# Normalising the second rows on VectorE, quantising layer 1 later, and both halves of a unit's probabilities on GpSimd one slot later

## The chip, the cores and the metric

The kernel runs on one core of one Trainium2 chip. The metric is the device time in microseconds (us). Before the change it is 1662.19 us, the median of 3 runs (1658.11 to 1663.67).

## What is computed

`x` is 32 batches of 256 rows by 256 features (float32); `ctx_768` has 77 context rows of 192 features for each batch. Two layers follow each other, each with an attention on the context and a feed-forward part. The feed-forward part of layer 0 is a gated one with integer weights; that of layer 1 quantises its rows to 8-bit integers.

```python
x = x + L0_xattn(_layernorm(x), ctx, Wq, Wk, Wv, Wo, bo)   # 16 heads of 64
x = x + L0_ffn(_layernorm(x), w_gate, w_up, w_down)        # 768 hidden, silu(gate) * up
x = x + L1_xattn(_layernorm(x), ctx, Wq, Wk, Wv, Wo, bo)
x = x + L1_ffn(_layernorm(x), rhs)
# L1_ffn(lhs): s = max|lhs| / 127 by row, r = max|rhs| / 127 by column
#              (round(lhs / s) @ round(rhs / r)) * s * r
```

## The kernel before, in words

A first part of some 200 us computes keys and values of all batches and both layers and stores them in DRAM. Then `h` runs over 64 steps (`NB`, layer 0 of the 32 batches, then layer 1 of the same), and two more for what is left. A step is one batch of one layer, in four slots `u` (called `UNITS`); a unit is four heads. In `lay`, `lay[d]` is the layer of step `h + d`, so that `lay[-2] == 0` means work that belongs to the batch two steps back, in layer 0. Each engine has its own `body` with the whole order of its slots written out by hand, and counting semaphores between the engines; no engine looks ahead past its next instruction.

What one unit k passes through:

- TensorE, slot k: the scores into one PSUM tile `SC`, once ScalarE has read those of the unit before (L1200). In the same slot it makes the queries of the unit two further on (L328), projects the unit four back into `OA` (L326, L328, once VectorE's `oT_l` is there) and weighs the values of the unit three back (L1234).
- VectorE, slot k: `maxima` of half 0 and of half 1 (L1507; a half is 128 of the 256 rows).
- ScalarE, slot k: `exponentials` of both halves (L1379) into `ex[k % 2]`, which must have been read by GpSimd two units before.
- VectorE: `reciprocals` of half 0 at the end of slot k, of half 1 at the start of slot k+1 (L1512).
- GpSimd: `probabilities`, three operations a half: `pr` = ex times reciprocal (L1668), its fp16 part `p` (L1681), the low part (L1673). Half 0 comes late in slot k, half 1 early in slot k+1. A half's `p` is turned by a DMA transpose that SyncE issues (L1090, L1091), in slot k+1.

At the end of slot 3, VectorE adds the residual and makes `x1` (L1648), the rows behind the attention. Before it may overwrite the old `x1` in layer 0 it waits for GpSimd's copy of it into `y` (L1710). Then the second rows are made: `spreads` and `moments` of `x1` on VectorE (L365, L371, L373, which gives `ve`), `inverse` on GpSimd (`rs`, L388), `shift` on VectorE (`nmr`, L378), `normalise` on ScalarE in two activations (`x2`, L347). In layer 0, ScalarE then takes the fp16 part (L343), VectorE the low part (L357, `x<-x`), SyncE turns both (L1099), and TensorE multiplies by the gate and up weights. GpSimd also takes the low part of four of six hidden tiles (`low_hidden`, L1659), adds the bias to `x_res` in layer 0 (L1692) and makes the inverses of the first and third norms.

In layer 1 the second rows go to VectorE's `am` (L1595, largest magnitude), `quantising_scale` (L1500, L1503), ScalarE's `q_a` (L1425), VectorE's `q_i` (L1588), TensorE's turn (L319), VectorE's `qiT` (L1615), TensorE's `quantised`, VectorE's `ya` (L1600) and `yo` (L1634), and a store of SyncE (L1151).

SyncE's queue is one list too: per step it holds eight transposes of `p`, two loads of keys (`load_keys`, L302: units 2 and 3 in slot 0, units 0 and 1 of the next batch in slot 2), two of values, the residual, and in layer 0 further transposes and stores. An issue waits behind all that are written before it.

## Time and profile before

| | us |
|---|---|
| median of 3 runs | 1662.19 |
| lowest and highest | 1658.11, 1663.67 |
| the profiled execution's own time | 1661.49 |
| its span in the trace | 1659.7 |
| granted TensorE clock, mean | 0.994 |

In the profile PE is TensorE's matmuls and PEld its weight loads (which overlap PE), DVE is VectorE, ACT ScalarE, POOL GpSimd, SP SyncE. A row gives the line of the kernel, the engine, the operation, output and inputs by name (buffer numbers left out) and the count. "Idle before" is the time for which the engine stood still just before the instruction, with what released it. The ends of matmuls are modelled, and neighbouring instructions of an engine may overlap by some 0.1 us, so that distances from start to start are the ones to add.

### The profile page before, as it was taken

How to read it: one execution, taken by the hardware profiler on the slowest of the kernel's cores; microseconds unless marked ns; L12 is line 12 of the kernel's file. 1: busy time of each engine (PE TensorE's matmuls, PEld its weight loads, DVE VectorE, ACT ScalarE, POOL GpSimd, SP SyncE). 2: the span in 40 equal slices, each digit the busy share in tenths (PEclk: the TensorE clock that was granted, in tenths of full speed). 3: DMA queues.
4: the chain of work that ended last, by engine and by line, in shares of the span. 5: the costliest groups of instructions: out<-in, count | busy, mean ns of one | idle time of the engine just before them, and what ended most of it. 6: DMA issues, size and time to landing. Idle time of an engine off the chain costs nothing.

```text
span 1659.7 us, 74850 instructions
## 1 busy us (share of the span) xinstructions
PE 1520.7 (92%) x27282; PEld 1318.8 (79%) x27282; DVE 1344.1 (81%) x3522; ACT 1372.0 (83%) x5640; POOL 1254.1 (76%) x1893
## 2 busy tenths in 40 slices
PE   7999889999999999999999999899999988999995
PEld 4556569889889889889889888777777777777774
DVE  6777668888888888888888878788888878888886
ACT  6656688888888888898898888888888888888884
POOL 5100288889889889889898888788888887888884
PEclk9999999999999999999999999999999999999998
DMA  9997699877787778778778988888888888888995
GB/s 260 348 307 263 193 205 175 170 171 179 163 171 180 164 169 179 163 170 176 170 168 176 163 171 153 163 180 176 177 183 185 184 178 177 181 175 176 178 186 112
DMA packets 740022, 307.78 MB, mean 185 GB/s; under 512 B 629201, under 2 KB 725361, under 8 KB 737841
## 3 DMA queue, kind: packets, MB, share of 16 engines
q1 hardware_dynamic: 738049, 299.32, 81.8%
q0 software_dynamic: 1840, 6.82, 1.4%
q8 instruction: 68, 1.11, 0.3%
q14 instruction: 65, 0.53, 0.1%
HBM read 87.09 MB, written 65.54 MB: 92 GB/s over the span
## 4 chain that ended last, share of the span: by engine, by line
ACT 23%; PE 21%; POOL 19%; DVE 11%; issue 10%; DMA 2%; SPq 1%; ACTq 1%; DVEq 0%; POOLq 0%
ACT ex L1379 15%; PE psum L328 14%; POOL pr L1668 6%; POOL p L1681 4%; ACT x L347 4%; PE psum L1234 3%; PE psum L1200 3%; DVE x L1648 2%; POOL p L1673 2%; DVE nmax L1507 2%; POOL hT_l L1659 2%; POOL rs L388 2%; POOL x_res L1692 2%; ACT q_a L1425 1%; DVE st L365 1%
## 5 line engine op out<-in xcount | busy, mean ns | idle before, releaser
L1379 ACT ACTIVATE ex<-psum,nmax 128x77 f32<-128x77 f32 x2048 | 636.3, 331 | 73.5 <-DVE nmax L1507 70.6
L1379 ACT ACTIVATION_READ_ACCUMULATOR ex<-psum,nmax 128x1 f32 x2048 | 432.5, 211 | 0.0
L1673 POOL TENSOR_TENSOR p<-pr,p 128x308 f16<-128x308 f32 x512 | 397.3, 776 | 38.5 <-ACT p L343 0.3
L1668 POOL TENSOR_TENSOR pr<-ex,rden 128x308 f32<-128x308 f32 x512 | 366.1, 715 | 67.1 <-DVE rden L1512 66.9
L328 PE MATMUL psum<-xT,wq_h 128*64 128x256 f16 x4064 | 353.0, 275 | 0.0
L328 PE MATMUL psum<-wo_h,oT_h 128*64 128x256 f16 x1792 | 249.6, 274 | 47.8 <-DVE oT_l L357 47.6
L1681 POOL CAST p<-pr 128x308 f16<-128x308 f32 x509 | 253.1, 497 | 38.2 <-DMA pT<-p 5.8
L328 PE MATMUL psum<-xT,wq_l 128*64 128x256 f16 x2032 | 280.8, 273 | 0.0
L1507 DVE TENSOR_REDUCE nmax<-psum 128x4 f32<-128x308 f32 x512 | 235.7, 461 | 22.5 <-PE psum L1200 20.6
L328 PE MATMUL psum<-wo_l,oT_h 128*64 128x256 f16 x1792 | 248.2, 273 | 0.0
L328 PE MATMUL psum<-wo_h,oT_l 128*64 128x256 f16 x1792 | 248.1, 273 | 0.0
L328 PEld LDWEIGHTS psum<-xT,wq_h 128*64 128x64 f16 x4064 | 211.0, 110 | 12.1
L1234 PE MATMUL psum<-pT,vb 77*64 77x256 f16 x3072 | 212.5, 273 | 0.0
L343 ACT ACTIVATE oT_h<-psum 128x512 f16<-128x512 f32 x256 | 152.5, 596 | 44.1 <-PE psum L1234 39.7
L357 DVE TENSOR_TENSOR oT_l<-psum,oT_h 128x512 f16<-128x512 f32 x256 | 174.5, 682 | 1.5 <-ACT oT_h L343 1.5
L360 DVE SCALAR_TENSOR_TENSOR qT_l<-psum,qT_h 128x512 f16<-128x512 f32 x256 | 173.6, 678 | 0.0
L1234 PEld LDWEIGHTS psum<-pT,vb 77*64 77x64 f16 x3072 | 167.2, 110 | 3.8 <-issue 0.4
L1200 PEld LDWEIGHTS psum<-kb,qT_h 64*128 64x128 f16 x4096 | 113.1, 94 | 65.4 <-issue 65.4
L1200 PE MATMUL psum<-kb,qT_h 64*128 64x77 f16 x4096 | 145.3, 197 | 11.3 <-ACT ex L1379 5.0
L343 ACT ACTIVATE qT_h<-psum 128x512 f16<-128x512 f32 x256 | 152.3, 595 | 2.9 <-PEq L398 2.9
L328 PEld LDWEIGHTS psum<-wo_h,oT_h 128*64 128x64 f16 x1792 | 102.2, 110 | 65.5 <-DVE oT_l L357 58.0
L388 POOL TENSOR_TENSOR rs<-ve,half_neg 128x2 f32<-128x2 f32 x127 | 88.4, 696 | 76.6 <-DVE ve L373 73.6
(164 smaller groups left out, 3484.2 us busy)
## 6 DMA issues: line engine op xcount, KB each, us to landing
keys<-ks SPq DMA_DIRECT2D x16, 1232.0 KB, 7.2
kb<-keys SPq DMA_DIRECT2D x256, 77.0 KB, 2.8
vb<-vals SPq DMA_DIRECT2D x128, 154.0 KB
vals<-vs SPq DMA_DIRECT2D x64, 256.0 KB, 4.0
x_pair<-in_x_dram SPq DMA_DIRECT2D x32, 256.0 KB, 3.0
pT<-p SPq DMA_TRANSPOSE x512, 3.3
x_res<-in_x_dram SPq DMA_DIRECT2D x32, 256.0 KB, 3.1
mid_x<-y SPq DMA_DIRECT2D x32, 256.0 KB, 2.4
```

Source lines behind the costliest of these rows:

```text
L328: last = pe.matmul(o[b * DH:(b + 1) * DH], w[:, b * DH:(b + 1) * DH], x, **flags)
L343: return act.activation(dst, src, ACT.Copy, scale=scale)
L357: return dve.tensor_tensor(dst, src, hi, ALU.subtract)
L360: return dve.scalar_tensor_tensor(out=qT_l[i][:, :, :], in0=src, scalar=Q_DOWN, in1=qT_h[i][:, :, :], op0=ALU.mult, op1=ALU.subtract)
L388: pool.tensor_tensor(rs[:, :], ve[:, :], half_neg[:, :], ALU.pow).then_inc(s_inv[k], 1)
L1200: last = pe.matmul(SC[:, b, at], w[rows, a, t * P:(t + 1) * P], kb[u // 2][rows, b, part, u % 2 * PPU + a, :], start=(q == 0), stop=(q == ...
L1234: last = pe.matmul(o[b * DH:(b + 1) * DH, a, :].rearrange("p (t q) -> p t q", q=P), vb[u // 2][:, part, c:c + DH], pT[u][0:NK, b, at:at + ...
L1379: last = act.activation(ex[i][:, t, b, :], SC[:, t, b * NK:(b + 1) * NK], ACT.Exp, bias=nmax[i][:, t, b:b + 1], accum_out=den[i][:, t, b:b ...
L1507: dve.tensor_reduce(nmax[i][:, t, :], SC[:, t, :].rearrange("p (h k) -> p h k", k=NK), AX_X, ALU.max, negate=True).then_inc(s_m, 1)
L1668: pool.tensor_tensor(pr[:, t, :, :], ex[i][:, t, :, :], r, ALU.mult).then_inc(s_p, 1)
L1673: pool.tensor_tensor(d[:, t, 1, :, 0:NK], pr[:, t, :, :], d[:, t, 0, :, 0:NK], ALU.subtract).then_inc(s_pl, 1)
L1681: pool.tensor_copy(p16[v % 2][:, t, 0, :, 0:NK], pr[:, t, :, :]).then_inc(s_ph, 1)
```

## The change

Five edits go together.

1. VectorE normalises the second rows itself, out of `mv` and `rs`, in two operations a batch, in both layers (`normalise_rows`). The `shift` on VectorE and the two activations on ScalarE go.
2. Layer 1's quantising moves later: `spreads` and `moments` of its `x1` go behind both maxima of slot 0, the normalising and `am` from slot 0 to slot 1, `q_a` and `q_i` from slot 1 to slot 2 (`q_a` ahead of the slot's queries and exponentials on ScalarE), the turn from slot 1 to slot 2, `quantised`, `ya` and `yo` from slot 2 to slot 3, the store to slot 0 of the next step. `x1` also waits for `yo`.
3. One reciprocal a unit, of both halves, at the start of slot k+1.
4. GpSimd does half 0 of unit k at the start of slot k+1 too, then half 1.
5. In layer 0 `inverse` of the second rows stays the last of slot 3 on GpSimd, right behind the copy into `y`, and half 0 of unit 3, which stood between the two, comes after it.

```diff
+        def normalise_rows(dve, k, dst, src, mv, rs, count, s_done):
+
+            dve.wait_ge(s_inv[k], count)
+            dve.sem_inc(s_stgo[k], 1)
+            for t in range(QT):
+                dve.tensor_scalar(dst[:, t, :], src[:, t, :], mv[:, t, 0:1], rs[:, t:t + 1], ALU.subtract,
+                                  ALU.mult).then_inc(s_done, 1)
...
@@ SyncE
+                        if u == 0 and lay[-3] == 1:
+                            store_output(h - 3 - B)
                         if u == 0 and lay[1] == 0 and like >= 4:
                             turn_rows(sp, h + 1, like + 1)
...
-                        if u == 3 and lay[-2] == 1:
-                            sp.wait_ge(s_ysum, h - 1 - B)
-                            sp.dma_start(batch_of(out_rows, b_out), yo[:, :, :]).then_inc(s_yo, 16)
@@ TensorE
-                        if u == 2 and lay[-2] == 1:
+                        if u == 3 and lay[-2] == 1:
                             pe.wait_ge(s_qe, h - 1 - B)
                             for t in range(QT):
                                 quantised(t, bank("quant", t))
...
-                        if u == 1 and lay[-2] == 1:
+                        if u == 2 and lay[-2] == 1:
                             pe.wait_ge(s_qi, h - 1 - B)
                             turn(pe, as_f16(bank("turned_q", 0)), q_i).then_inc(s_qt, 1)
@@ ScalarE
+                        if u == 2 and lay[-2] == 1 and like <= NB:
+                            act.wait_ge(s_li, h - 1 - B)
+                            after(act, s_qi, h - 2 - B)
+                            for t in range(QT):
+
+                                act.activation(q_a[:, t, :], x2[:, t, :], ACT.Copy, scale=linv[:, t:t + 1],
+                                               bias=MAGIC).then_inc(s_qa, 1)
...
-                        if u == 0 and lay[-2] is not None and like <= NB:
-                            act.wait_ge(s_nmr[1], h - 1)
-                            if lay[-2] == 0 or like == B + 2:
-                                after(act, s_x216l, h - 2)
-                            normalise(act, x2, x1, rs2, 1, s_x2)
@@ VectorE
-                    def reciprocals(k, i, t):
-                        dve.wait_ge(s_e, QT * k + t + 1)
-                        dve.reciprocal(rden[i][:, t, :], den[i][:, t, :]).then_inc(s_r, 1)
+                    def reciprocals(k, i):
+                        dve.wait_ge(s_e, QT * k + 2)
+                        dve.reciprocal(rden[i][:, :, :], den[i][:, :, :]).then_inc(s_r, 1)
...
+                        if u == 0 and lay[-2] == 1:
+                            dve.wait_ge(s_x1, h - 1)
+                            spreads(dve, x1, st2, s_st2)
                             moments(dve, 1, st2, mv2, ve2, s_st2, s_mv2, h - 2)
...
-                        if u == 0 and lay[-2] is not None and like <= NB:
-                            shift(dve, 1, mv2, rs2, h - 1)
+                        if u == 0 and lay[-2] == 0:
+                            normalise_rows(dve, 1, x2, x1, mv2, rs2, h - 1, s_x2)
...
+                        if u == 1 and lay[-2] == 1 and like <= NB:
+                            normalise_rows(dve, 1, x2, x1, mv2, rs2, h - 1, s_x2)
...
-                        if lay[0] is not None:
-                            reciprocals(n + u, u % 2, 0)
...
+                            if lay[-2] == 1:
+                                dve.wait_ge(s_ysum, h - 1 - B)
@@ GpSimd
                     for u in range(UNITS):
                         if u == 0 and lay[-3] == 0:
                             low_hidden(2, h - 3)
+                        if lay[(u - 1) // UNITS] is not None and (like, u) != (NB, 0):
+                            probabilities(h + (u - 1) // UNITS, (u - 1) % UNITS, 0)
...
-                        if (like, u) == (NB - 1, 3):
-                            weights_of(h, 3, 0)
-                            low_of(h, 2, 1)
-                        elif lay[0] is not None:
-                            probabilities(h, u, 0)
...
-                        if u == 3 and lay[-1] == 0:
+                        if u == 3 and lay[-1] is not None:
                             inverse(pool, 1, ve2, rs2, h)
```

## Rows read from the trace of the kernel before

**Rows 1.** The page, first part: busy time, share of the span, instructions.

```profile
PE 1520.7 (92%) x27282; PEld 1318.8 (79%) x27282; DVE 1344.1 (81%) x3522; ACT 1372.0 (83%) x5640; POOL 1254.1 (76%) x1893
```

**Rows 2.** L1648 (x1), in 300 to 900 and 1100 to 1600: min/median/max ns, first, last start.

```profile
L1648 DVE SCALAR_TENSOR_TENSOR x<-psum,x_res x24: 690/692/693, 308.3 to 886.9; 128x512 f32<-128x512 f32 x24
...
L1648 DVE SCALAR_TENSOR_TENSOR x<-psum,x_res x26: 690/692/692, 1105.0 to 1594.3; 128x512 f32<-128x512 f32 x26
```

**Rows 3.** Who waited for whom, 300 to 900 us (layer 0): total us, times, longest.

```profile
PE psum L328 <- DVE oT_l L357: 25.7, 24, 1.2
...
POOL hT_l L1659 <- ACT hT_h L343: 27.7, 24, 1.2
...
POOL rs L388 <- DVE ve L373: 12.1, 24, 0.8
```

**Rows 4.** The same view, 1100 to 1600 us (layer 1).

```profile
PE psum L319 <- DVE q_i L1588: 19.5, 25, 0.8
...
PE psum L326 <- DVE oT_l L357: 17.2, 25, 0.7
...
PE psum L328 <- DVE oT_l L357: 10.0, 26, 0.4
```

**Rows 5.** GpSimd in order of time, layer 0: start us, us, what, idle before.

```profile
609.03 0.61 POOL L1710 COPY y<-x 128x512 f32<-128x512 f32 x1
609.62 0.70 POOL L1668 TENSOR_TENSOR pr<-ex,rden 128x308 f32<-128x308 f32 x1
...
612.40 0.69 POOL L388 TENSOR_TENSOR rs<-ve,half_neg 128x2 f32<-128x2 f32 x1 [0.74 <-DVE ve L373]
...
629.20 0.89 POOL L1681 CAST p<-pr 128x308 f16<-128x308 f32 x1
...
634.41 0.61 POOL L1710 COPY y<-x 128x512 f32<-128x512 f32 x1
```

**Rows 6.** VectorE in order of time, layer 0.

```profile
629.11 0.69 DVE L357 TENSOR_TENSOR x<-x_pair,x 128x512 f16<-128x512 f32 x1
...
635.16 0.69 DVE L1648 SCALAR_TENSOR_TENSOR x<-psum,x_res 128x512 f32<-128x512 f32 x1 [0.24 <-POOL y L1710]
...
637.27 0.17 DVE L373 TENSOR_SCALAR ve<-mv 128x2 f32<-128x2 f32 x1
```

**Rows 7.** Groups of instructions by form, 300 to 900 us: count, busy us, mean ns.

```profile
L1681 POOL CAST p<-pr 128x308 f16<-128x308 f32 x191 | 104.7, 548 | 12.3
...
L378 DVE SCALAR_TENSOR_TENSOR nmr<-mv,rs 128x2 f32<-128x2 f32 x71 | 30.7, 432 | 4.6 <-POOL rs L388 4.6
```

**Rows 8.** L767, the one earlier use of VectorE's normalising form.

```profile
L767 DVE TENSOR_SCALAR x_pair<-x_pair,mv,rs x2: 404/405/406, 166.3 to 166.6; 128x256 f32<-128x256 f32 x2
```

**Rows 9.** ScalarE in order of time, both layers: normalising and q_a.

```profile
614.66 1.09 ACT L347 ACTIVATE x<-x,nmr,rs 128x256 f32<-128x256 f32 x2
...
1309.76 0.91 ACT L1425 ACTIVATE q_a<-x,linv 128x256 f32<-128x256 f32 x2
```

**Rows 10.** TensorE in order of time, layer 1: first scores of slots 1, 2, 3 and 0.

```profile
1305.76 0.25 PE L1200 MATMUL psum<-kb,qT_h 64*128 64x77 f16 x4
...
1312.53 0.25 PE L1200 MATMUL psum<-kb,qT_h 64*128 64x77 f16 x4
...
1316.89 0.24 PE L1200 MATMUL psum<-kb,qT_h 64*128 64x77 f16 x4
...
1320.83 0.24 PE L1200 MATMUL psum<-kb,qT_h 64*128 64x77 f16 x4
```

**Rows 11.** SyncE's queue in order of time, and landing of the keys, layer 1.

```profile
1311.82 1.24 SPq L1091 DMA_TRANSPOSE pT<-p  x1
1313.11 1.23 SPq L302 DMA_DIRECT2D kb<-keys  x2
...
DMA to landing us min/median/max: 2.3/2.8/4.3
```

**Rows 12.** One batch of layer 1: busy us of PE, PEld, DVE, ACT, POOL; clock; DMA.

```profile
1300.71:1320.28 19.57, 17.69 (x344) 15.41 (x342) 15.88 (x41) 16.80 (x79) 15.95 (x26) 1.00 0.80 180
```

More of the change, by code:

```diff
@@ L1004, in uses @@
                         out.append(("gu", 0))
-                    if lay[-2] == 1:
-                        out.append(("turned_q", 0))
                 if u == 2:
@@ L1009, in uses @@
                         out.append(("down", 0))
-                    if lay[-2] == 1:
-                        out += [("quant", 0), ("quant", 1)]
                     if lay[-3] == 0:
@@ L1015, in uses @@
                         out.append(("gu", 1))
+                    if lay[-2] == 1:
+                        out.append(("turned_q", 0))
+                if u == 3 and lay[-2] == 1:
+                    out += [("quant", 0), ("quant", 1)]
                 if u == 3 and lay[-2] == 0:
@@ L1419, in body @@
                             exponentials(n + u, u % 2, 0)
-                        if u == 1 and lay[-2] == 1 and like <= NB:
-                            act.wait_ge(s_li, h - 1 - B)
-                            after(act, s_qi, h - 2 - B)
-                            for t in range(QT):
-                                act.activation(q_a[:, t, :], x2[:, t, :], ACT.Copy, scale=linv[:, t:t + 1],
-                                               bias=MAGIC).then_inc(s_qa, 1)
                         if u == 1 and lay[1] == 1:
@@ L1531, in body @@
                         if lay[(u - 1) // UNITS] is not None:
-                            reciprocals(n + u - 1, (u - 1) % 2, 1)
+                            reciprocals(n + u - 1, (u - 1) % 2)
                         if lay[0] is not None:
                             maxima(n + u, u % 2, 0)
-                        if u == 0 and lay[-2] is not None:
+                        if u == 0 and lay[-2] == 0:
+                            moments(dve, 1, st2, mv2, ve2, s_st2, s_mv2, h - 2)
+                        if u == 2 and lay[-2] == 0:
+                            hidden(0, h - 2)
+                        if u == 2 and lay[-3] == 0:
+                            out_rows(0)
+                        if u == 2 and lay[2] == 0:
+                            shift(dve, 0, mv1, rs1, h + 2)
+                        if lay[-1] is not None:
+                            dve.wait_ge(s_oh, n + u - 3)
+                            low(dve, oT_l[u % 2][:, :, :], weighed(like, u), oT_h[u % 2][:, :, :]).then_inc(s_ol, 1)
+                        if u == 2 and lay[-2] == 1:
+                            dve.wait_ge(s_qa, QT * (h - 1 - B))
+                            after(dve, s_qt, h - 2 - B)
+                            dve.tensor_scalar(q_i[:, :, :], q_a[:, :, :], MAGIC + INT8_MAX, MAGIC,
+                                              ALU.min, ALU.subtract).then_inc(s_qi, 1)
+                        if lay[0] is not None:
+                            maxima(n + u, u % 2, 1)
+                        if u == 0 and lay[-2] == 1:
+                            dve.wait_ge(s_x1, h - 1)
+                            spreads(dve, x1, st2, s_st2)
                             moments(dve, 1, st2, mv2, ve2, s_st2, s_mv2, h - 2)
@@ L1553, in body @@
                                                   ALU.add).then_inc(s_qa, 1)
-                        if u == 2 and lay[-2] == 0:
-                            hidden(0, h - 2)
-                        if u == 2 and lay[-3] == 0:
-                            out_rows(0)
-                        if u == 2 and lay[2] == 0:
-                            shift(dve, 0, mv1, rs1, h + 2)
-                        if lay[-1] is not None:
-                            dve.wait_ge(s_oh, n + u - 3)
-                            low(dve, oT_l[u % 2][:, :, :], weighed(like, u), oT_h[u % 2][:, :, :]).then_inc(s_ol, 1)
-                        if lay[0] is not None:
-                            maxima(n + u, u % 2, 1)
                         if late_tile(like, u) is not None:
@@ L1584, in body @@
                             sigmoid_gate(4, h - 3)
-                        if u == 1 and lay[-2] == 1:
-                            dve.wait_ge(s_qa, QT * (h - 1 - B))
-                            after(dve, s_qt, h - 2 - B)
-                            dve.tensor_scalar(q_i[:, :, :], q_a[:, :, :], MAGIC + INT8_MAX, MAGIC,
-                                              ALU.min, ALU.subtract).then_inc(s_qi, 1)
                         if lay[(u + 1) // UNITS] is not None:
@@ L1607, in body @@
                                 turned_rows(like + 1, 0)).then_inc(s_xl, 1)
-                        if u == 1 and lay[-1] == 1:
+                        if u == 1 and lay[-2] == 1 and like <= NB:
+                            dve.wait_ge(s_x2, QT * (h - 1))
+                            dve.tensor_reduce(am[:, :], x2[:, :, :], AX_X, ALU.max,
+                                              apply_absolute_value=True).then_inc(s_am, 1)
+                            quantising_scale(h - 2 - B)
+                        if u == 2 and lay[-1] == 1:
                             dve.wait_ge(s_xr, 16 * h)
@@ L1611, in body @@
                             dve.tensor_tensor(x_res[:, :, :], x_res[:, :, :], bias, ALU.add).then_inc(s_xb, 1)
-                        if u == 1 and lay[-2] == 1:
+                        if u == 2 and lay[-2] == 1:
                             dve.wait_ge(s_qt, h - 1 - B)
```

27 lines of the change are left out of this document (12 added, 15 removed).

## The prediction

> **What bounds the kernel now.** The page comes first: TensorE is busy for 92% of the span, ScalarE 83%, VectorE 81%, GpSimd 76% [rows 1]. Shares of the whole hide that there are two stages with different work a step, so the next look is at the starts of x1, one a step. In layer 0 they lie (886.9 - 308.3) / 23 = 25.16 us apart, in layer 1 (1594.3 - 1105.0) / 25 = 19.57 us [rows 2]. Some 31 steps run at the first pace and some 28 at the second, so a microsecond a step is worth about 30 us.
>
> Then the waits, stage by stage. In layer 0 TensorE stands still for 25.7 / 24 = 1.07 us a step, for VectorE's oT_l [rows 3]. But it isn't what closes the loop: GpSimd hardly ever rests. It waits 1.15 us a step for a hidden tile of ScalarE and 0.50 us for ve [rows 3], so its own work, gaps included, is 25.16 - 1.65 = 23.5 us a step. And x1 of each step stands until GpSimd has copied the old x1 into y: 0.24 us of idle with that releaser [rows 6]. The reader is to see a ring there: the copy into y, x1, statistics, ve, GpSimd's inverse, and round GpSimd's list to the next copy.
>
> In layer 1 no copy is made. There TensorE's three waits are 0.75 us for q_i, 0.66 us and 0.38 us for oT_l (19.5, 17.2 and 10.0 over 26 steps) [rows 4]: 1.80 us a step, and without them a step is 17.77 us, in line with 17.69 us of busy TensorE [rows 12].
>
> **Part by part, layer 0.** *Normalising.* ScalarE loses a pair of 1.09 us [rows 9], VectorE loses a shift of 0.43 us [rows 7] and gains two operations of the form of 0.40 us, whose starts lie 0.3 us apart [rows 8], so 0.3 to 0.4 us net. As the pair stands ahead of the fp16 part of the rows, of oT_h and of the hidden tile, these come about 1 us earlier against x1. That takes away TensorE's 1.07 us and GpSimd's 1.15 us as causes. The four reciprocals that go give VectorE 0.1 us each, as it isn't the bound: nothing.
>
> *GpSimd's order.* This is the part that costs. Before, between the copy into y and the inverse stood half 0 of unit 3: from 609.62 until the idle of 0.74 us that ends at 612.40, so 2.04 us [rows 5]. In this time VectorE made x1 and its statistics: the copy ends at 634.41 + 0.61 = 635.02, ve at 637.27 + 0.17 = 637.44 [rows 5, 6], 2.4 us, and in the batch before, copy to inverse took 612.40 - 609.64 = 2.76 us [rows 5]. The half covered it but for 0.50 us on average. After the change the inverse stands right behind the copy. The copy holds up x1, x1 holds up ve, ve holds up the inverse, and GpSimd's whole list of the next step, half 0 of unit 3 first, is queued behind it. GpSimd rests 2.4 to 2.8 us a step, and the step is its work plus this rest: 23.5 + 2.5 = 26.0 us, where 2.5 us is the half's 2.04 plus the mean wait of 0.50. That is +0.84 us a step, and over 31 steps **+26 us**. Below, it could be +0.4 if fewer of GpSimd's operations meet VectorE's (a cast takes 0.89 us beside a VectorE subtraction, 0.548 us on average [rows 5, 6, 7]); above, +1.1 from 2.76 us, and more under the third rival.
>
> What is late behind it: probabilities of unit 3 by about 4 us against x1, the other units less. Their values are weighed three slots, some 18 us, later, and two GpSimd passes stand between a buffer of ex and its next use. I take nothing for it. TensorE gains slack of 2 us a step that the loop doesn't let it use.
>
> On the SBUF port the trace shows that cast of 0.89 us, begun at 629.20 within VectorE's subtraction of 629.11 [rows 5, 6]. The Trainium skill, GPSIMD Engine Reference, section Specifications, says that GpSimd's SBUF interfaces are shared with VectorE and contend with its instructions that have two SBUF inputs or run in a 2-port mode. The trace agrees for the two inputs; by the rule the added normalising would speak against this change, and the third rival prices it.
>
> **Layer 1.** *ScalarE's pair and the early wait.* VectorE no longer stands for x2 ahead of slot 1's maxima, and its statistics come behind both maxima of slot 0, so that oT_l of slots 0 and 1 is ready before TensorE asks: 0.38 + 0.66 us. q_i is now made a slot earlier than TensorE turns it, which takes 0.75 us. Full worth 1.80 us.
>
> *What q_a costs at its new place.* The distances of the scores are 6.77 us for slot 1, 4.36 for slot 2, 3.94 for slot 3 [rows 10], and 19.57 less these for slot 0, 4.50. Slot 3 is what maxima, 16 exponential instructions and two fp16 copies allow, since TensorE may write the next scores only after them. In slot 2, q_a comes between these: 0.8 to 0.91 us [rows 9] makes 4.65 to 4.85, against TensorE's own some 4.3 there (quantised leaves, a turn of about the same length comes). So 0.4 us a step is handed back: 17.77 + 0.4 = 18.15 us, -1.42 us a step, over 28 steps **-40 us**. Bounds: -1.80 (q_a fits) and -0.67 (the second rival). quantised in slot 3 and the turn in slot 2 are work of equal length moved: nothing. yo and the extra wait of x1 for it lie on VectorE's own list, ahead of x1 already, and there x1 had to wait for TensorE anyway: nothing. The store goes behind one transpose in slot 0 of the next step and delays the values' load by its issue, about 0.6 us; values are used two slots on.
>
> *GpSimd in layer 1.* Its 15.95 us [rows 12] and gaps, some 17, fit into 18.15, but ve now comes behind both maxima and unit 3 waits behind the inverse. An estimate, from the start of slot 0's scores: 0.6 us for them, 1.4 for VectorE's two maxima and oT_l, 1.2 for statistics and ve (of the 2.4 above, without x1 and one of the maxima), so ve at 3.2 us, the inverse until 3.9, and halves of 2.0 us: half 0 of unit 0, the third, ends at 9.9 us, half 1 at 11.9. In SyncE's queue the keys of the next batch's first units stand behind that half's transpose. I get 13.2 us for their issue (11.9 plus 1.24 [rows 11]), their second load 0.6 later, landing 2.8 us on, so 16.6 us of 18.15: covered by 1.5 us.
>
> **Ends.** At the change of layers steps are of mixed kind; nothing. At the last step GpSimd finds two more operations of 0.7 to 0.75 us behind the last reciprocal: +1.5 us.
>
> **Sum.** Against the profiled execution's own 1661.5 us (0.7 below the median of 1662.19): 1661.5 + 26 - 40 + 1.5 = **1649 us**. About 0.3%, 5 us, is what a measurement of this kernel tells from no change.
>
> **Rivals.** *First, TensorE is the bound in both layers.* The Trainium skill, Perfetto Trace Analysis, section Identifying the Most-Contended Engine, calls the engine of highest occupancy the one to work on (for TensorE by weight loads rather than by matmul time). Worked from rows, the mechanism is that the loop through GpSimd has play that I don't see, and layer 0 gives back TensorE's 1.07 us: -33 us there, -1.80 x 28 = -50 in layer 1, 1580 us. For it: TensorE's 92%. Against it: x1's wait for the copy, and GpSimd's list, whose order leaves nothing to hide 2.5 us. Chance 0.08.
>
> *Second, the other side: the keys come late.* Place: SyncE's queue in slot 1 and 2 of layer 1. If a half takes GpSimd 2.2 us in place of 2.0 (0.8 us by half 1 of unit 0) and the keys land at the slow end, 4.3 us [rows 11], the first scores wait until 16.6 + 0.8 + 1.5 = 18.9 us. Layer 1 gains 0.67 x 28 = 19 us, layer 0 loses 26: 1661.5 + 26 - 19 + 1.5 = 1670 us. It decides from the point where a step of layer 1 is longer than 19.57 - 26/28 = 18.6 us. For it: a DMA share of 0.80 [rows 12] that rises as the step shrinks. Against it: the median landing. Chance 0.12.
>
> *Third, port contention.* Each normalising pair meets GpSimd in its fullest stretch and lengthens it by its own 0.6 to 0.7 us: 21 us more in layer 0, 1670 us. For it: that cast; against it: a form that has no case beside a busy GpSimd. Chance 0.10.
>
> **Numbers.** The forecast has 0.60, with 1632 to 1662 as its own range (layer 0 +12 to +34, layer 1 -50 to -32). The remaining 0.10 is for layer 0 losing less than bounded, or a gain of layer 1 that stops at q_i alone, 0.75 us. Range 1620 to 1673: it leaves out the first rival. Faster by over 0.3%: 0.69 (most of the forecast, the first rival, a little of the rest); within 0.3%: 0.12; slower: 0.19 (second and third rival without their mild cases).
>
> **What would show it.** In layer 0: x1 starts 26.0 us apart; GpSimd idle 2.4 to 2.8 us before its inverse, for ve, in every step, and no more for the hidden tile; VectorE's x1 waiting for the copy by over 0.5 us. In layer 1: starts 18.15 us apart, no wait of TensorE for q_i, slot 2 longer than TensorE's work, ScalarE's q_a without idle ahead of it. I am wrong if layer 0's distance falls, if TensorE waits for the keys, or if GpSimd's casts grow beside the normalising pair.

## The result: slower by 1.9%, and the profile after

| | before | after |
|---|---|---|
| median, us | 1661.41 (4 runs) | 1691.93 (4 runs) |
| lowest and highest | 1658.11 to 1663.67 | 1688.96 to 1700.91 |
| ratio | | 1.0194, 95% interval 1.0149 to 1.024 |
| profiled execution: time, span | 1661.49, 1659.7 | 1688.96, 1687.2 |

The forecast was 1649 us. The change makes the kernel slower by 30 us, and the time lies above the range. The page of the changed kernel, first part (busy us, share, instructions), beside [rows 1]:

```profile
PE 1536.4 (91%) x27282; PEld 1318.8 (78%) x27282; DVE 1396.8 (83%) x3329; ACT 1314.8 (78%) x5514; POOL 1265.3 (75%) x1893
```

ScalarE is relieved by 57 us and VectorE loaded with 53 us more, although it has 193 instructions fewer. Shares still say little; the distances of x1 say where the time is. x1 of the changed kernel, in 300 to 900 us and in 1130 to 1630 us (min/median/max ns, first and last start), beside [rows 2]:

```profile
L1659 DVE SCALAR_TENSOR_TENSOR x<-psum,x_res x23: 690/691/692, 311.3 to 889.1; 128x512 f32<-128x512 f32 x23
...
L1659 DVE SCALAR_TENSOR_TENSOR x<-psum,x_res x26: 691/692/693, 1135.8 to 1619.5; 128x512 f32<-128x512 f32 x26
```

Layer 0: (889.1 - 311.3) / 22 = 26.26 us a step, forecast 26.0. Layer 1: (1619.5 - 1135.8) / 25 = 19.35 us, forecast 18.15. All 63 distances added up, the first 34 (layer 0 and the change of layers) grew from 854.6 to 886.2 us, +31.6; the other 29 went from 562.9 to 559.0 us, -3.9. The first x1 comes 0.2 us earlier, and the stretch behind the last is the same, 11.4 us. So layer 0 lost what was forecast and a little more, and layer 1 gave 4 us where 40 were forecast.

**Layer 0.** Waits of the changed kernel, 300 to 900 us (total us, times, longest), beside [rows 3]:

```profile
POOL rs L396 <- DVE ve L381: 69.0, 46, 2.5
...
DVE x L1659 <- POOL y L1725: 31.6, 23, 1.4
```

GpSimd in order of time, one turn of the ring (start us, us, what, idle before), beside [rows 5], and VectorE in the same stretch, beside [rows 6]:

```profile
619.96 1.07 POOL L396 TENSOR_TENSOR rs<-ve,half_neg 128x2 f32<-128x2 f32 x1 [0.50 <-DVE ve L381]
...
625.74 0.61 POOL L1725 COPY y<-x 128x512 f32<-128x512 f32 x1
628.85 0.69 POOL L396 TENSOR_TENSOR rs<-ve,half_neg 128x2 f32<-128x2 f32 x1 [2.50 <-DVE ve L381]
```

```profile
626.49 0.69 DVE L1659 SCALAR_TENSOR_TENSOR x<-psum,x_res 128x512 f32<-128x512 f32 x1 [1.38 <-POOL y L1725]
...
628.60 0.17 DVE L381 TENSOR_SCALAR ve<-mv 128x2 f32<-128x2 f32 x1
```

The reader sees the ring as the prediction drew it: copy 625.74, x1 626.49, ve 628.60, inverse 628.85, and nothing of GpSimd's between copy and inverse. GpSimd rests 2.50 us there in every step, its wait for the hidden tile is gone, and x1 waits 1.38 us for the copy. There is one rest more, 0.50 us ahead of another inverse in the list, that of the third norm: 69.0 / 23 = 3.0 us a step in all.

**Layer 1.** Waits of the changed kernel, 1130 to 1630 us, beside [rows 4]:

```profile
POOL rs L396 <- DVE ve L381: 42.5, 26, 1.7
...
DVE nmax L1513 <- PE psum L1211: 36.6, 55, 1.7
...
PE psum L328 <- DVE oT_l L357: 20.6, 46, 0.6
ACT q_a L1424 <- DVE linv L1509: 20.1, 23, 0.9
```

TensorE's wait for q_i is gone, as forecast, and for the keys it waited a single time, 0.7 us. But VectorE now stands 36.6 / 26 = 1.4 us a step for scores, waits that were 0.2 us before, and yet is late elsewhere. VectorE in order of time at the seam of two steps of layer 1:

```profile
1344.87 0.48 DVE L1513 TENSOR_REDUCE nmax<-psum 128x4 f32<-128x308 f32 x1 [0.53 <-PE psum L1211]
...
1346.85 0.86 DVE L1604 SCALAR_TENSOR_TENSOR ya<-psum,lsc,rhs_sb 128x256 f32<-128x256 f32 x2
1347.84 1.27 DVE L1643 TENSOR_TENSOR yo<-ya,x 128x512 f32<-128x512 f32 x1
1349.25 0.69 DVE L1659 SCALAR_TENSOR_TENSOR x<-psum,x_res 128x512 f32<-128x512 f32 x1
...
1350.31 0.68 DVE L357 TENSOR_TENSOR oT_l<-psum,oT_h 128x512 f16<-128x512 f32 x1
```

and TensorE's first scores of slot 3 and then of slots 0, 1, 2 and 3 of the next step, beside [rows 10]:

```profile
1344.25 0.25 PE L1211 MATMUL psum<-kb,qT_h 64*128 64x77 f16 x4 [0.32 <-ACT ex L1390]
...
1348.62 0.24 PE L1211 MATMUL psum<-kb,qT_h 64*128 64x77 f16 x4
...
1353.52 0.25 PE L1211 MATMUL psum<-kb,qT_h 64*128 64x77 f16 x4 [0.32 <-DVE qT_l L360]
...
1358.16 0.24 PE L1211 MATMUL psum<-kb,qT_h 64*128 64x77 f16 x4
...
1363.76 0.25 PE L1211 MATMUL psum<-kb,qT_h 64*128 64x77 f16 x4 [0.40 <-ACT ex L1390]
```

ya and yo fill VectorE from 1346.85 to 1349.11. x1 starts right behind them, without any wait for TensorE, 0.63 us after the scores of slot 0 have begun, and oT_l and the maxima of slot 0 stand behind x1. Before, x1 had waited for TensorE.

The same rows tell where in the step the time went. From score to score, slot 0 lasts 4.90 us here, slot 1 4.64 and slot 2 5.60. The medians over layer 1 are 4.75, 4.64, 5.53 and 4.37 us for slots 0 to 3, against 4.50, 6.77, 4.37 and 3.93 before. So slot 1 gave 2.1 us; slot 2, into which the quantising moved, took 1.2 us of it back, slot 3 0.4 and slot 0 0.25.

### The profile page after: what moved, and what is told of

Read it like the earlier page. It is cut to its first block, busy times and chain, and to the rows that moved or that the text cites. A ratio compares the mean times of both kernels' runs of the same rounds, so it can differ in the third digit from the quotient of the medians.

```text
span 1687.2 us, 74557 instructions
## 1 busy us (share of the span) xinstructions
PE 1536.4 (91%) x27282; PEld 1318.8 (78%) x27282; DVE 1396.8 (83%) x3329; ACT 1314.8 (78%) x5514; POOL 1265.3 (75%) x1893
## 3 DMA queue, kind: packets, MB, share of 16 engines
q8 instruction: 68, 1.11, 0.3%
## 4 chain that ended last, share of the span: by engine, by line
POOL 42%; issue 25%; DVE 11%; PE 3%; ACT 3%; DMA 2%; SPq 1%; DVEq 0%; POOLq 0%; ACTq 0%
POOL pr L1679 16%; POOL p L1692 10%; POOL p L1684 6%; POOL hT_l L1670 4%; POOL x_res L1705 2%; POOL rs L396 2%; ACT ex L1390 2%; DVE nmax L1513 2%; DVE oT_l L357 2%; DVE qT_l L360 2%; PE psum L328 1%; DMA pT<-p 1%; DVE yo L1643 1%; PE psum L1211 1%; POOL y L1725 1%
## 5 line engine op out<-in xcount | busy, mean ns | idle before, releaser
L1679 POOL TENSOR_TENSOR pr<-ex,rden 128x308 f32<-128x308 f32 x512 | 380.3, 743 | 20.7 <-DVE rden L1518 20.4
L1692 POOL CAST p<-pr 128x308 f16<-128x308 f32 x509 | 246.4, 484 | 36.5 <-DMA pT<-p 4.0
L396 POOL TENSOR_TENSOR rs<-ve,half_neg 128x2 f32<-128x2 f32 x127 | 98.0, 772 | 185.5 <-DVE ve L381 185.4
L1245 PEld LDWEIGHTS psum<-pT,vb 77*64 77x64 f16 x3072 | 165.0, 110 | 15.8 <-issue 13.0
```

The source lines that it names most:

```text
L396: pool.tensor_tensor(rs[:, :], ve[:, :], half_neg[:, :], ALU.pow).then_inc(s_inv[k], 1)
L1245: last = pe.matmul(o[b * DH:(b + 1) * DH, a, :].rearrange("p (t q) -> p t q", q=P), vb[u // 2][:, part, c:c + DH], pT[u][0:NK, b, at:at + ...
L1679: pool.tensor_tensor(pr[:, t, :, :], ex[i][:, t, :, :], r, ALU.mult).then_inc(s_p, 1)
L1692: pool.tensor_copy(p16[v % 2][:, t, 0, :, 0:NK], pr[:, t, :, :]).then_inc(s_ph, 1)
```

## The experiments

In the expectations, R is the theory that the ring of layer 0 sets its step, V that VectorE's list sets that of layer 1, Q that q_a's place does. The table has the mean distance of x1, in steps 4 to 26 (layer 0) and 37 to 60 (layer 1), and the ratio to the kernel before where both were timed several times; the others have the one time of their profiled execution.

| kernel | layer 0 | layer 1 | us | ratio, interval |
|---|---|---|---|---|
| before | 25.16 | 19.57 | 1661.41 | |
| after | 26.27 | 19.34 | 1691.93 | 1.0194, 1.0149 to 1.024 |
| e1 after, GpSimd's old order | 24.55 | 19.08 | 1640.85 | 0.9876, 0.9848 to 0.9904 |
| e2 before, GpSimd's new order | 26.09 | 19.57 | 1693.27 | 1.019, 1.0158 to 1.0221 |
| e3 after, copy ahead of half 1 | 25.53 | 19.34 | 1674.41 | 1.0084, 1.0056 to 1.0113 |
| e4 after, no normalising in layer 1 | 26.30 | 18.12 | 1660.84 | |
| e5 after, that pair twice | 26.27 | 20.04 | 1719.76 | |
| e6 after, no yo | 26.27 | 18.81 | 1677.63 | |
| e7 after, q_a behind exponentials | 26.27 | 19.32 | 1694.35 | 1.0211, 1.0167 to 1.0255 |
| e8 e1, bias on GpSimd | 24.56 | 19.07 | 1638.80 | 0.9857, 0.9834 to 0.9879 |
| e9 e1, layer 1's pair on ScalarE | 24.59 | 19.91 | 1661.94 | 0.9987, 0.9973 to 1.0001 |
| e10 e1, layer 0's pair on ScalarE | 25.16 | 19.06 | 1655.41 | |
| e11 before, edit 1 alone | 24.55 | 18.30 | 1608.58 | 0.9651, 0.9614 to 0.9689 |
| e12 before, edit 1 in layer 0 alone | 24.56 | 19.57 | 1646.66 | 0.9873, 0.9833 to 0.9912 |
| e13 e11, product and yo in slot 3 | 24.58 | 19.16 | 1634.80 | |
| e14 e11, statistics late | 24.58 | 20.50 | 1678.80 | |
| e15 e1, statistics early | 24.56 | 19.39 | 1645.95 | |

### GpSimd's order: e1, e2, e3

e1 undoes edits 3, 4 and 5 in the changed kernel.

```diff
-                        if lay[(u - 1) // UNITS] is not None and (like, u) != (NB, 0):
-                            probabilities(h + (u - 1) // UNITS, (u - 1) % UNITS, 0)
+                        if u == 3 and lay[-1] == 1:
+                            inverse(pool, 1, ve2, rs2, h)
+                        elif lay[0] is not None:
+                            probabilities(h, u, 0)
...
+                        if lay[0] is not None:
+                            reciprocals(n + u, u % 2, 0)
```

> The changed kernel with GpSimd's old order and the two old reciprocals a unit; normalising on VectorE and the later quantising stay. Theory R (a ring in layer 0: copy into y, x1, ve, inverse, with nothing of GpSimd's between copy and inverse): layer 0 falls from 26.27 us a step to 24.2 to 24.7, since half 0 of unit 3 stands between them again and ScalarE's pair is gone. Theory P (the normalising pair beside a busy GpSimd costs layer 0 its time): layer 0 stays over 25.5. Layer 1 by both near 19.4, because its limit is thought to be VectorE's list. In all 1625 to 1645 us by R, over 1665 by P.

e2 is the other side: the kernel before with edits 3 to 5 alone.

> The kernel before with GpSimd's new order and one reciprocal a unit, and nothing else. R: layer 0 goes from 25.14 to about 26.0 us a step, GpSimd resting some 2.5 us ahead of the inverse of the second rows. P: layer 0 stays within 0.2 us of 25.14. Layer 1: its inverse comes at once after slot 3, unit 3 waits behind it: 19.6 to 19.9 us a step. In all 1685 to 1700 us by R, 1660 to 1670 by P.

e1: layer 0 fell to 24.55 us, 1.72 us below the changed kernel, and the whole is faster than before. e2: the new order alone gives +0.93 us a step in layer 0, nothing in layer 1, and a ratio of 1.019, the whole slowdown. The only wait of GpSimd in layer 0 (300 to 900 us of e2) is the one for ve, twice a step as in the changed kernel:

```profile
POOL rs L388 <- DVE ve L373: 69.0, 46, 2.5
```

The order is the cause in layer 0; both sides agree. They move edits 3, 4 and 5 together, and no run parts the single reciprocal from the order of GpSimd's list.

e3 keeps the new order but puts the copy into y one half earlier, so that a half stands between copy and inverse again.

```diff
+                        if u == 3 and lay[-2] == 0:
+                            ...
+                            pool.tensor_copy(y[:, :, :], x1[:, :, :]).then_inc(s_yx, 1)
                         if (like, u) == (NB - 1, 3):
                             weights_of(h, 2, 1)
```

> The changed kernel with one move: in slot 3 of layer 0 GpSimd copies x1 into y ahead of half 1 of unit 2, so that this half stands between copy and inverse. R: layer 0 falls from 26.27 to 24.2 to 24.8 us a step and GpSimd rests at most 0.6 us before that inverse. P: it stays over 25.8. Layer 1 as in the changed kernel, 19.4. In all 1625 to 1650 us by R.

25.53 us: a miss. The rest ahead of the second norm's inverse fell only from 2.50 to 1.63 us. GpSimd and TensorE of e3, order of time and waits, 300 to 900 us:

```profile
622.94 0.69 POOL L396 TENSOR_TENSOR rs<-ve,half_neg 128x2 f32<-128x2 f32 x1 [1.63 <-DVE ve L381]
```

```profile
PE psum L328 <- POOL hT_l L1670: 17.6, 23, 0.8
```

With the halves a slot later in GpSimd's list, its low part of a hidden tile comes later too, and TensorE's down projection waits 0.77 us a step for it, a wait that the kernel before doesn't have (the changed kernel has it too, 16.6 / 22 = 0.75 us). The chain of waits of e3 goes from there over the third norm to the copy into y. So the order binds in a second place, which the prediction did not name. That this second loop sets e3's 25.53 us is read from the chain; no run took it away.

### Layer 1 as a sum of VectorE's work: e4 to e8

The theory at this point: VectorE's list bounds layer 1, and what was added to it costs its length. e4 leaves out layer 1's normalising (am and q_a read x1 itself), e5 does the pair a second time into a buffer of its own, e6 leaves out the addition of x1 to layer 1's product.

```diff
 e5
+                            for t in range(QT):
+                                dve.tensor_scalar(x2b[:, t, :], x1[:, t, :], mv2[:, t, 0:1], rs2[:, t:t + 1],
+                                                  ALU.subtract, ALU.mult).then_inc(s_dbl, 1)
 e6
-                            dve.tensor_tensor(yo[:, :, :], ya[:, :, :], x1[:, :, :], ALU.add).then_inc(s_ysum, 1)
+                            dve.sem_inc(s_ysum, 1)
```

> The changed kernel without the normalising of the second rows of layer 1 (row maximum and quantising read x1 itself), all waits kept. Theory V (VectorE's list bounds layer 1): a step of layer 1 falls from 19.4 us by most of the pair's 1.2 to 1.4 us, to 18.0 to 18.5. Theory Q (the place of q_a on ScalarE ahead of slot 2's exponentials, or the keys, bound it whatever VectorE does): it falls by less than 0.5 us. Layer 0 unchanged at 26.27.

> The changed kernel with the normalising pair of layer 1 done twice, the first time into a tile of its own. V (VectorE's list bounds layer 1, and a pair beside GpSimd takes 1.2 to 1.4 us): a step of layer 1 goes from 19.35 to 20.5 to 20.8 us. If the pair's port contention were not what costs it (uncontended pair, 0.7 us): 20.0. Theory Q (VectorE isn't the bound): under 19.8.

> The changed kernel without yo, the addition of x1 to layer 1's product (the product alone is stored); ya and all waits stay. V: the 1.27 us that yo takes ahead of x1 go from VectorE's list; a step of layer 1 falls from 19.35 by 0.5 to 1.2 us, and x1 starts right behind TensorE's projection. Q: under 0.3 us.

Without the pair layer 1 is 1.22 us faster, without yo 0.53 us; with the pair twice 0.70 us slower, half of what the theory asked. Part of the asymmetry lies in lsc, an operation of 128x2, behind the pair: groups of 1130 to 1630 us in the changed kernel, of 1150 to 1600 in e4 and in e5:

```profile
L368 DVE TENSOR_SCALAR x<-x,mv,rs 128x256 f32<-128x256 f32 x52 | 35.5, 721 | 0.0
L1643 DVE TENSOR_TENSOR yo<-ya,x 128x512 f32<-128x512 f32 x26 | 29.7, 1143 | 3.1
...
L1506 DVE TENSOR_SCALAR lsc<-am 128x2 f32<-128x2 f32 x26 | 16.4, 632 | 0.9
```

```profile
L1645 DVE TENSOR_TENSOR yo<-ya,x 128x512 f32<-128x512 f32 x25 | 19.9, 795 | 3.0
...
L1506 DVE TENSOR_SCALAR lsc<-am 128x2 f32<-128x2 f32 x24 | 4.3, 180 | 0.8
```

```profile
L1508 DVE TENSOR_SCALAR lsc<-am 128x2 f32<-128x2 f32 x23 | 3.9, 170 | 0.8
```

lsc is 0.63 us in the changed kernel and 0.17 to 0.18 us in both others: they shift it against GpSimd's work. yo falls from 1.14 to 0.80 us in e4 as well. The last section comes back to that.

e7 puts q_a behind the first exponentials of slot 2 (q_i and the turn follow it down), e8 gives layer 1's bias (0.80 us) to GpSimd in e1.

```diff
 e7
-                        if u == 2 and lay[-2] == 1 and like <= NB:
-                            ... q_a ahead of the slot's queries
                             exponentials(n + u, u % 2, 0)
+                        if u == 2 and lay[-2] == 1 and like <= NB:
+                            ... q_a
 e8
-                        if u == 2 and lay[-1] == 0:
+                        if u == 2 and lay[-1] is not None:
```

> The changed kernel with q_a behind the first four exponentials of slot 2 on ScalarE, q_i behind the slot's low part of the queries on VectorE, and the turn behind the weighing on TensorE. Q (q_a, which waits 0.87 us for its scale ahead of the queries' copy and all exponentials of slot 2, costs layer 1 its time): a step falls from 19.35 to 18.3 to 18.7 us. V: by at most 0.3 us.

> The kernel of e1 (old order of GpSimd) with layer 1's bias of x_res on GpSimd in slot 2, as in layer 0, in place of VectorE. V: VectorE's list is 0.7 to 0.9 us shorter and GpSimd's rest of 1.3 us takes most of the 1.27 us it gets: a step of layer 1 falls from 19.08 to 18.3 to 18.7 us, in all 1618 to 1632 us. Q: unchanged at 19.1, or longer if GpSimd's list of 18.3 us comes to bound it.

e7: 19.32 against 19.34 us. q_a's wait for its scale, and its place ahead of the first exponentials, cost nothing. But e7 leaves q_a in slot 2, between the exponentials of its two halves, and slot 2 stays at 5.48 us (median); what quantising in that slot costs, e7 does not say. e8: 19.07 against 19.08 us, a miss. 0.8 us of VectorE's work taken out of slot 2 changes nothing, while the pair of slot 1 and yo of slot 3 counted. So it isn't the sum of VectorE's list that bounds layer 1; the part of it that lies in certain slots counts. e8 says one thing more: GpSimd's work grew by 0.8 us a step and its wait for ve shrank as much, so GpSimd had play in layer 1 of e1 and wasn't what closed its loop.

### Who should normalise: e9 and e10

e9 takes e1 and gives layer 1's pair back to ScalarE, late; the scale, q_a, q_i and the turn come later too. e10 takes e1 and gives layer 0's pair back.

```diff
 e9, in ScalarE's body, behind the second exponentials of slot 1
+                        if u == 1 and lay[-2] == 1 and like <= NB:
+                            act.wait_ge(s_nmr[1], h - 1 - B)
+                            ...
+                            normalise(act, x2, x1, rs2, 1, s_x2)
```

> e1 (GpSimd's old order, the two old reciprocals) with layer 1's normalising given back to ScalarE, but at its new, late time: the shift of the mean on VectorE in slot 1, the two activations at the end of slot 1 behind the exponentials, the largest magnitude and the scale on VectorE in slot 2, q_a behind the first exponentials of slot 2, q_i and the turn later in the slot. All of the computation is done. Theory V, VectorE's list bounds layer 1: a pair of 1.4 us leaves it and a shift of about 0.4 us comes; by the 1.23 us a step that leaving the pair out gave, less 0.4 us for the shift, layer 1's step goes from 19.08 to 18.0 to 18.5 us, layer 0 stays at 24.5, and the whole is 1615 to 1630 us. Theory S, ScalarE is full once VectorE is relieved: the pair of 1.1 us on it comes between two slots' exponentials and the step stays at 19.0 or more, 1640 us and up.

> e1 with layer 0's normalising given back to ScalarE (shift on VectorE, two activations on ScalarE, as before the change). If the gain of e1 in layer 0 (25.16 to 24.55 us a step) is the normalising on VectorE, as the prediction had it, this kernel's layer 0 is at 25.1 to 25.2 us and layer 1 at 19.1, about 1659 us. If the gain comes from elsewhere, such as layer 1's edits or the order of VectorE's list, layer 0 stays at 24.5 to 24.7 us and the whole at 1641 us.

e10: 25.16 us, to the hundredth the distance of the kernel before. Edit 1 is worth 0.61 us a step in layer 0.

e9: layer 1 went up to 19.91 us. The number that theory S named was reached, but ScalarE is not full: it is busy for 403.8 of 480 us in layer 1 (1120 to 1600 us), in e1 for 400.4. VectorE of e9 in order of time, a little over one step:

```profile
1349.54 0.69 DVE L1666 SCALAR_TENSOR_TENSOR x<-psum,x_res 128x512 f32<-128x512 f32 x1
...
1360.81 0.68 DVE L1559 TENSOR_REDUCE am<-x 128x2 f32<-128x512 f32 x1
...
1363.10 0.90 DVE L1609 TENSOR_SCALAR q_i<-q_a 128x512 f16<-128x512 f32 x1 [0.52 <-ACT q_a L1436]
...
1365.03 0.41 DVE L1631 TENSOR_SCALAR qiT<-psum 128x512 f16<-128x512 f16 x1
...
1368.23 0.91 DVE L1614 SCALAR_TENSOR_TENSOR ya<-psum,lsc,rhs_sb 128x256 f32<-128x256 f32 x2 [0.69 <-PE psum L328]
...
1369.27 0.69 DVE L1650 TENSOR_TENSOR yo<-ya,x 128x512 f32<-128x512 f32 x1
1370.10 0.69 DVE L1666 SCALAR_TENSOR_TENSOR x<-psum,x_res 128x512 f32<-128x512 f32 x1
```

x1, statistics, normalising, am, scale, q_a, q_i, turn, qiT, product, ya, yo and then x1 of the next step: since x1 waits for yo, the whole quantising of a batch must fit into one step. Made late at its start, the chain is waited for at its end: TensorE waits for q_i in every step, 24.9 / 23 = 1.1 us (1120 to 1600 us). The wait of ya for the product, 0.69 us in the step shown, occurs in only 4 steps. Theory V fell. Of S, it is not shown that ScalarE's time bounds the step; whether the pair costs by standing between the exponentials of two slots, or by making the chain late, e9 does not part. What the run points to is edit 2 itself, which made that chain end at x1.

### Edit 2 taken apart: e11 to e15

e11 is the kernel before with edit 1 alone, in both layers, e12 the same in layer 0 only.

```diff
 e11
-                            act.wait_ge(s_nmr[1], h - 1)
-                            ...
-                            normalise(act, x2, x1, rs2, 1, s_x2)
...
-                            shift(dve, 1, mv2, rs2, h - 1)
+                            normalise_rows(dve, 1, x2, x1, mv2, rs2, h - 1, s_x2)
```

> The kernel before, with edit 1 alone, in both layers: VectorE normalises the second rows, where its shift stood in slot 0; the order of layer 1's quantising, the reciprocals and GpSimd's order stay as before. All of the computation is done. Layer 0: the prediction's first part says that TensorE's wait of 1.07 us and GpSimd's of 1.15 us for the hidden tile go; by e1 and e10 the step comes to 24.5 to 24.6 us. Layer 1: the pair costs VectorE 1.4 us a step and saves it the stand for ScalarE's pair of 1.1 us, so by theory V without edit 2 the step is 19.4 to 19.8 us, and edit 2 is worth some 0.5 us of e1's 19.08. If instead edit 2 is what costs in layer 1 (a longer chain through the quantising now that x1 waits for yo), layer 1 comes to 18.6 us or less here, and the whole under 1620 us. Theory V: 1640 to 1655 us.

> The kernel before, with edit 1 alone and in layer 0 only; layer 1 is as before the change in every instruction. All of the computation is done. If the two layers are independent, layer 0 is at 24.5 to 24.6 us a step and layer 1 at 19.57, about 1643 to 1648 us; edit 2 with its late quantising would then be worth only what e1 has beyond that, 5 us or less. If layer 0's gain in e1 needed the late quantising too, layer 0 stays at 25.1 us and the time at 1661 us.

e11 is the fastest kernel of the study: 1608.58 us, ratio 0.9651. Layer 1 is at 18.30 us without edit 2, against 19.08 us with it, so edit 2 **costs** 0.78 us a step where the prediction had counted on it for most of its gain. The two layers are independent: e12 has 24.56 and 19.57 us. Waits of layer 1 in the kernel before (1110 to 1580 us) and in e11 (1110 to 1560 us):

```profile
DVE am L1595 <- ACT x L347: 33.9, 24, 1.4
...
PE psum L319 <- DVE q_i L1588: 18.8, 24, 0.8
```

```profile
DVE x L1651 <- PE psum L328: 14.5, 24, 0.6
...
PE psum L328 <- DVE oT_l L365: 9.3, 24, 0.4
PE psum L319 <- DVE q_i L1591: 8.1, 25, 0.6
```

VectorE's wait of 1.4 us for ScalarE's pair is gone, q_i comes earlier by it, and TensorE's wait for it falls from 0.8 to 0.3 us. That is the gain the prediction wanted from a later slot; normalising on VectorE gives it by itself.

Which part of edit 2 costs? e13 moves only the product, ya and yo to slot 3 of e11, with x1's wait for yo; e14 moves only the statistics behind both maxima; e15 takes e1 and moves the statistics back.

```diff
 e13, the same in TensorE's, SyncE's and VectorE's bodies
-                        if u == 2 and lay[-2] == 1:
+                        if u == 3 and lay[-2] == 1:
...
                             after(dve, s_x2, QT * (h - 1))
+                            if lay[-2] == 1:
+                                dve.wait_ge(s_ysum, h - 1 - B)
 e14
                             maxima(n + u, u % 2, 1)
+                        if u == 0 and lay[-2] == 1 and like <= NB:
+                            dve.wait_ge(s_x1, h - 1)
+                            spreads(dve, x1, st2, s_st2)
+                            moments(dve, 1, st2, mv2, ve2, s_st2, s_mv2, h - 2)
```

> e11 (the kernel before with edit 1 alone; layer 1 at 18.30 us a step) with one part of edit 2: quantised, ya and yo go from slot 2 to slot 3, x1 waits for yo, and the store goes to slot 0 of the next step. Everything else of layer 1's quantising stays where it was. All of the computation is done. Theory Y, what costs is that ya and yo, over 2 us of VectorE's time with the gaps, stand in slot 3 ahead of x1, on which slot 0's product waits: layer 1 goes to 18.8 to 19.1 us. Theory T (the statistics' place) and theory N (the pair's place in slot 1) say that it stays at 18.2 to 18.4 us.

> e11 with another part of edit 2: layer 1's statistics of x1 (spreads and moments) go behind both maxima of slot 0, the normalising stays in slot 0 behind them. All of the computation is done. Theory T, the late ve makes GpSimd wait before its inverse and passes this on through its list: layer 1 at 18.8 us or more. Theories Y and N: 18.2 to 18.5 us.

> e1 (all of edits 1 and 2, GpSimd's old order; layer 1 at 19.08 us) with the statistics of layer 1 back at their old place ahead of slot 0's maxima; the rest of edit 2 stays. All of the computation is done. Theory T: layer 1 falls to 18.3 to 18.5 us. Theories Y and N: it stays at 18.9 to 19.2 us, as the rest of edit 2 is still there. If e13 stays at 18.3 and this kernel at 19, the pair's and the quantising's later place is what costs (theory N).

e13: 19.16 us, +0.86. That part alone costs as much as all of edit 2. VectorE of e11 and then of e13 in slots 2 and 3:

```profile
1318.24 0.86 DVE L1603 SCALAR_TENSOR_TENSOR ya<-psum,lsc,rhs_sb 128x256 f32<-128x256 f32 x2
...
1319.23 0.97 DVE L1637 TENSOR_TENSOR yo<-ya,x 128x512 f32<-128x512 f32 x1
...
1320.33 0.48 DVE L1510 TENSOR_REDUCE nmax<-psum 128x4 f32<-128x308 f32 x1
```

```profile
1314.58 0.18 DVE L1518 RECIPROCAL rden<-den 128x4 f32<-128x4 f32 x1 [0.97 <-ACT ex L1390]
1315.33 0.48 DVE L1513 TENSOR_REDUCE nmax<-psum 128x4 f32<-128x308 f32 x1 [0.57 <-PE psum L1211]
...
1317.30 0.87 DVE L1606 SCALAR_TENSOR_TENSOR ya<-psum,lsc,rhs_sb 128x256 f32<-128x256 f32 x2
...
1318.30 0.69 DVE L1640 TENSOR_TENSOR yo<-ya,x 128x512 f32<-128x512 f32 x1
1319.13 0.69 DVE L1656 SCALAR_TENSOR_TENSOR x<-psum,x_res 128x512 f32<-128x512 f32 x1
```

In e11 ya and yo fill the end of slot 2. In e13 VectorE idles there, 0.97 + 0.57 us, and slot 3 holds 1.83 us more ahead of x1 (1317.30 to 1319.13). In e11 x1 waits 14.5 / 24 = 0.60 us for TensorE, so slot 3 had no more than that to give; 1.83 - 0.60 = 1.2 us more than it could hide, of which 0.86 us came out in the step. e13 also moves TensorE's product, some 0.6 us of matmuls, to slot 3 ahead of its projection, and no run parts the two; e6, which takes yo alone out of slot 3 and gains 0.53 us, speaks for VectorE's share.

e14: 20.50 us, also worse, by 2.2 us: the normalising, still in slot 0, stands behind the late statistics, and the queries' low part (qT_l) behind it. In the step shown GpSimd waits 2.74 us before its inverse, and VectorE then 0.93 us for rs; TensorE waits 54.8 / 24 = 2.3 us a step for that low part (1110 to 1600 us):

```profile
1305.14 1.16 DVE L350 TENSOR_SCALAR x<-x,mv,rs 128x256 f32<-128x256 f32 x2 [0.93 <-POOL rs L396]
```

The granted clock in layer 1 of this one execution was 0.95, against 1.00 in e13, so a part of the 2.2 us may be the clock's.

e15: 19.39 us, so in the company of the late normalising the late statistics are worth 0.3 us rather than costing anything. The statistics aren't the cause. All the rest of edit 2 beside e13's part, which is the later statistics, normalising, q_a, q_i and turn, comes out near nothing together (e1 19.08, e13 19.16). It is not nothing slot by slot: from e13 to e1 the medians of slots 0 to 3 go from 5.27, 5.36, 4.15 and 4.37 to 4.32, 4.64, 5.53 and 4.37 us. What slots 0 and 1 gain, slot 2 takes back.

## Why the prediction was wrong

**Edit 2, the failed step.** The prediction said of yo and x1's extra wait that "there x1 had to wait for TensorE anyway: nothing". The wait was real but only 0.60 us long, and what was put in front of it is 1.83 us. e13 measures what was priced at nothing with +0.86 us, 24 us over 28 steps. A cover was named and its length not held against what it had to cover.

**Edit 1 in layer 1, right in kind, given to the wrong edit.** The 1.80 us of TensorE's waits were credited to edits 1 and 2 together. Edit 1 alone yields 1.27 us (e11), over two thirds of it. The sum of 18.15 us for a step is nearly met by e11, 18.30 us; what the change adds to edit 1 spoils it.

**q_a in slot 2, 0.4 us: too small, and not for the reason given.** The slot was to last 4.65 to 4.85 us (the prediction's own terms, 3.94 + 0.80, give 4.74 at the low end) and lasts 5.53 us, 1.16 us over the 4.37 of the kernel before. q_a's wait for its scale is not what does it, since e7 took that away and found 0.02 us; what does is open. Against e13 slots 0 and 1 give as much back, so that this term does not decide the sum.

**The pair, 0.3 to 0.4 us net: too small.** Its form took 0.40 us in [rows 8], where GpSimd was idle; in layer 1 it takes 0.72 us on average, 1.43 us for the pair, and leaving it out gave 1.22 us (e4, with 0.45 us less for lsc and 0.35 us less for yo in it). It was priced from the one row that has no neighbour. That in itself would not have turned the sign: e11 pays for it and gains.

**GpSimd's order, layer 0: right.** The ring, its members, x1's wait and the sign are as forecast, and e1 and e2 show from both sides that the order is the cause. Mis-sized is the rest: 3.0 us for "2.4 to 2.8", since the third norm's ve costs 0.50 us too. GpSimd's work is 26.27 - 3.00 = 23.27 us, forecast 23.5. So 31.6 us for 26, the change of layers with it.

**Edit 1 in layer 0, priced together with the order.** The prediction let the 1.15 us for the hidden tile vanish, and by its working edit 1 without the new order would have been 23.5 + 0.5 = 24.0 us. It is 24.56 us (e12): two waits of 0.50 and 0.35 us, the second of them what is left of that for the hidden tile, and 23.7 us of work.

**GpSimd's order in layer 1.** From e1 to the changed kernel 19.08 to 19.34 us: 0.26 us a step that the prediction saw only as a risk to the keys. In e2, beside ScalarE's pair, it costs nothing.

**Ends.** The stretch behind the last x1 is unchanged, so the 1.5 us for GpSimd's two operations are not there; but the last distance of x1 grew from 15.5 to 19.2 us. It did so in e1, e9 and e15 (18.3 to 19.8 us) and not in e2 and e13 (15.6 and 15.8), so it comes with the late normalising and q_a.

**Sum.** Layer 1 -1.27 (edit 1), +0.78 (edit 2), +0.26 (GpSimd's order) = -0.23 us a step; layer 0 -0.61 (edit 1), +1.72 (order) = +1.11 us.

**The rivals.** The first, TensorE as the bound, fell: TensorE is busy for 91% and the order of a GpSimd busy for 75% sets layer 0. The trace speaks against the rule of the Trainium skill, Perfetto Trace Analysis, section Identifying the Most-Contended Engine, that was weighed there: taken by weight loads, as it asks, TensorE was at 79% before and ScalarE the highest with 83%, and GpSimd is the lowest by either count. The second, late keys, gave 1670 us, 22 us short, by a mechanism that is not there: TensorE waited for keys once. The third gave 1670 us too and said that the pair lengthens GpSimd's work in layer 0 by 0.6 to 0.7 us a step; it does by 0.2 us (23.1 us in e2, 23.3 in the changed kernel; 23.5 before, 23.7 in e12). None named the work put ahead of x1.

## What to carry to other kernels

Where a step is said to be hidden by a wait, put the two lengths side by side: work moved into a slot costs what it has over the wait that stood there, and the slot it left may only idle. When a late result hurts, first make it earlier at its source; moving its consumers a slot later also moves the end of its chain, and here that end stood ahead of the operation that starts the next step. And where an in-order engine both feeds and awaits another, look at what stands between the two in its list: that stretch of its own work is the cover.

## What the hardware showed that was not expected

Some of VectorE's operations grow in steps, by what GpSimd does beside them. In the changed kernel's layer 1 (1130 to 1630 us) lsc, 128x2, took 0.69 us in 23 of 26 cases, all begun 0.08 us after GpSimd's low part of the probabilities, and 0.17 us in the other three, begun when its product of ex and rden had 0.12 us left to run; in e11 (1110 to 1560 us) it stands at that same place in 23 of 24 steps and takes 0.17 us. GpSimd of the changed kernel and VectorE in order of time:

```profile
1358.69 0.75 POOL L1684 TENSOR_TENSOR p<-pr,p 128x308 f16<-128x308 f32 x1
```

```profile
1358.77 0.69 DVE L1506 TENSOR_SCALAR lsc<-am 128x2 f32<-128x2 f32 x1
```

lsc, begun 0.08 us later, ends at 1359.46, as GpSimd's operation does (1359.44): it was not slowed down but held to its end. The normalising, 0.40 us with GpSimd idle, took 0.57 to 0.61 us for its first and 0.91 us for its second operation in 23 of 26 steps, 0.40 and 0.53 us in the other three, and yo (0.69 us at best) takes up to 1.27 us. It goes both ways: in the seam above, yo runs from 1347.84 to 1349.11, and GpSimd's product, begun at 1348.52, took 1.15 us for 0.70. The Trainium skill, SBUF — State Buffer, section Who interferes with whom, says that the port pair shared by VectorE and GpSimd is an exclusive lock for a whole instruction, and that the order of issue decides who blocks. The trace agrees: lsc, begun second, was held, and so was GpSimd's product, begun second beside yo. What counts is how much of the neighbour is left. Beside the product of ex and rden lsc mostly began 0.12 us before its end, less than its own 0.17 us, and showed nothing; in the one step of e11 in which it began 0.14 us after the product had, with 0.56 us still to run, it took 0.59 us. The first normalising of e11's pair, begun with 0.50 us of the product left, takes 0.65 us.

This also says how such an operation is to be priced: not by its own length alone, but by what is left of the neighbour that it may have to stand behind.
